# Attention and a mixture of experts on one core: loads, key product and weight splits of the beginning in another order

## What is computed

```
x = x + tanh(g_xattn) * xattn(layernorm(x), context, mask)
x = x + tanh(g_ffn)   * moe(layernorm(x))

xattn: q = hs @ Wq.T + bq; k = ctx @ Wk.T + bk; v = ctx @ Wv.T + bv    (16 heads of 32)
       p = softmax(clip(where(mask, q.k / sqrt(32), -1e4), -50, 50))
       delta = clip(residual_scale, 0, 0.3) * ((p @ v) @ Wo.T + bo)
       layernorm(delta) * gamma + beta
moe:   8 experts, top 2 of softmax(x @ gate.T), renormalised;
       hidden = silu(gate part) * up part (1024), y = hidden @ down.T, sum of weight * y
```

## Time and profile before

| | |
|---|---|
| runs (us) | 964.10, 967.33, 969.12; median 967.33 |
| profiled execution | 964.62 us, span 962.9 us |
| mean granted clock of PE | 0.973 |
| busy, share of the span | PE 94%, DVE 45%, ACT 40%, POOL 27% |
| chain that ended last | PE 76%, issue 6%, POOL 6%, DVE 5%, ACT 3%, DMA 2% |
| moved by DMA | 93.93 MB, mean 98 GB/s |

### The profile page before, as it was taken

How to read it: one execution, slowest core, us unless ns; L and a number is a source line. 1 busy time by engine, 2 the same in 40 slices (tenths; PEclk the granted TensorE clock), 3 DMA queues, 4 the chain that set the end, 5 groups by cost and what they waited for, 6 DMA issues and landing times.

```text
span 962.9 us, 14512 instructions
## 1 busy us (share of the span) xinstructions
PE 903.6 (94%) x4267; PEld 723.8 (75%) x4268; DVE 434.9 (45%) x793; ACT 381.9 (40%) x733; POOL 262.7 (27%) x326
## 2 busy tenths in 40 slices
PE   4977999988789999999999999999999999999994
PEld 3755777766668888888888888888888888888883
DVE  5657868577692122532532534512532163226211
ACT  3565666642522222532532534422532262235221
POOL 6143737363231211211211221311221221112111
PEclk9999999997779999999999999999999999999997
DMA  7210131214744121461361463521361154121121
GB/s 312 88 45 0 60 116 57 74 61 159 265 169 138 33 33 22 121 206 22 117 210 22 118 209 109 207 33 22 110 217 22 33 185 131 30 36 22 27 38 22
DMA packets 27907, 93.93 MB, mean 98 GB/s; under 512 B 5425, under 2 KB 5425, under 8 KB 21105
## 3 DMA queue, kind: packets, MB, share of 16 engines
q1 hardware_dynamic: 18528, 72.03, 20.1%
q0 software_dynamic: 8640, 20.62, 11.7%
q10 hardware_dynamic: 720, 1.07, 0.3%
HBM read 75.03 MB, written 18.68 MB: 97 GB/s over the span
## 4 chain that ended last, share of the span: by engine, by line
PE 76%; issue 6%; POOL 6%; DVE 5%; ACT 3%; DMA 2%; DVEq 0%; SPq 0%; POOLq 0%; ACTq 0%
PE bank L254 69%; PE bank L1442 3%; POOL ex_lo L775 2%; PE bank L1428 2%; DMA xs<-in_x 2%; POOL o_lo L755 1%; POOL xr L759 1%; PE bank L1278 1%; DVE xr L419 1%; ACT hs L929 1%; DVE st_a L359 1%; DVE o_lo L559 0%; PE bank L1272 0%; POOL rs L763 0%; DVE tok_tile L642 0%
## 5 line engine op out<-in xcount | busy, mean ns | idle before, releaser
L254 PE MATMUL bank<-g_hi,gt_hi 128*128 128x512 f32 x592 | 237.5, 401 | 0.9 <-DVE gt_lo L668 0.9
L254 PE MATMUL bank<-g_lo,gt_hi 128*128 128x512 f32 x592 | 234.1, 395 | 0.0
L254 PE MATMUL bank<-g_hi,gt_lo 128*128 128x512 f32 x592 | 234.1, 395 | 0.0
L698 DVE TENSOR_TENSOR hid<-silu,bank 128x256 f32<-128x256 f32 x148 | 61.3, 419 | 307.4 <-ACT silu L1155 307.4
L1155 ACT ACTIVATE silu<-bank 128x256 f32<-128x256 f32 x148 | 56.5, 381 | 253.8 <-PE bank L254 253.8
L887 POOL COPY g_idx<-slot_idx 128x1 int32 x37 | 6.9, 185 | 470.1 <-ACT w_nxt L1169 470.1
L254 PEld LDWEIGHTS bank<-g_hi,gt_lo 128*128 128x128 f32 x592 | 111.3, 188 | 26.9
L254 PEld LDWEIGHTS bank<-g_hi,gt_hi 128*128 128x128 f32 x592 | 111.3, 188 | 26.3 <-issue 1.1
L254 PEld LDWEIGHTS bank<-g_lo,gt_hi 128*128 128x128 f32 x592 | 111.4, 188 | 25.0
L254 PE MATMUL bank<-dn_hi,hd_hi 128*128 128x512 f32 x296 | 126.8, 428 | 0.0
L254 PE MATMUL bank<-dn_hi,hd_lo 128*128 128x512 f32 x296 | 116.9, 395 | 0.0
(11 more groups left out here) (227 smaller groups left out, 1277.9 us busy)
## 6 DMA issues: line engine op xcount, KB each, us to landing
raw<-in_w_exp SPq DMA_DIRECT2D x48, 1024.0 KB, 5.3
raw<-in_w_attn SPq DMA_DIRECT2D x4, 1024.0 KB, 13.1
xs<-in_x SPq DMA_DIRECT2D x4, 1024.0 KB, 6.4
xr<-in_x SPq DMA_DIRECT2D x4, 1024.0 KB, 5.9
out_rows<-xr SPq DMA_DIRECT2D x16, 256.0 KB, 2.2
h_rows<-dh SPq DMA_DIRECT2D x16, 256.0 KB, 2.1
rows<-in_b_rows ACTq DMA_DIRECT2D x1, 1024.0 KB, 11.9
c_raw<-in_ctx_t SPq DMA_DIRECT2D x1, 640.0 KB, 3.9
```

The source lines that it names most:

```text
L254: mm = eng.matmul(psum, a(k), b(k), start=(first and k == 0 and j == 0), stop=(last and k == n - 1 and j == 2))
L698: dve.tensor_tensor(hid[:, p, :], silu[:, p, :], bank[p][:, 256:512], ALU.mult).then_inc(hid_done, 1)
```

## The change

- SP loads the key weights as four chunks of 128 x 512 with a semaphore each. The order is then value weights, xs, query weights, `rows`, output weights. `rows` was on ACT's queue, with the constants; it has its own semaphore now, and the wait for the constants counts four loads.
- ACT and DVE split the key weights chunk by chunk, and PE multiplies chunk by chunk, with four accumulations open at once in banks 0, 1, 6 and 7 (quarters m of the output). The key bias becomes four instructions of 256 columns, and the x transposes into banks 0 and 1 wait for the first two of them.
- PE starts with 36 transposes of the identity into bank 3, as soon as the identity is written; the wait for the rest of POOL's set-up moves behind the key product.
- The x transposes of batch 0 stand behind the third and the fourth value group (before: the first and the second).
- ACT splits the query weights ahead of normalise_x(0) (before: between the halves of x_high), DVE ahead of the value biases (before: after two x_low).
- The products of `rows` with the gates stand behind the first two clips, `bo_two` behind the last q_low of batch 0, and PE waits for it only after batch 0.
- In batch 0 ACT's o_copy(0) and o_copy(1) stand one exponential earlier; the split of the output weights stands behind k_high(1) on ACT, and ahead of v_low(1) and the last two q_low on DVE.

The value weights, the tiles and their sizes, the expert loop and all that is computed stay.

```diff
@@ sync @@
-            for w in range(2):
-                sp.dma_start(raw[:, w, :], w_attn[w]).then_inc(wload[w], 16)
+            for k in range(KC):
+                sp.dma_start(raw[:, 0, k * H:(k + 1) * H], w_attn[0][:, k * H:(k + 1) * H]).then_inc(
+                    wk_load[k - 1] if k else wload[0], 16)
+            sp.dma_start(raw[:, 1, :], w_attn[1]).then_inc(wload[1], 16)
             sp.dma_start(xs[:, :, :], x_b[0]).then_inc(xload, 16)
-            for w in range(2, 4):
-                sp.dma_start(raw[:, w, :], w_attn[w]).then_inc(wload[w], 16)
+            sp.dma_start(raw[:, 2, :], w_attn[2]).then_inc(wload[2], 16)
+            sp.dma_start(rows[:, :, :], b_rows.partition_broadcast(P)).then_inc(row_load, 16)
+            sp.dma_start(raw[:, 3, :], w_attn[3]).then_inc(wload[3], 16)
@@ vector, batch @@
+                if not back:
+                    split_weight(3)
+                if front:
                     v_low(b + 1)
                     q_low(b + 1, 2)
                     q_low(b + 1, 3)
-                if not back:
-                    split_weight(3)
@@ vector, beginning @@
-            split_weight(0)
+            for k in range(KC):
+                dve.wait_ge(wk_h, k + 1)
+                dve.tensor_tensor(wk_lo[:, k, :], raw[:, 0, k * H:(k + 1) * H], f32(wk_hi[:, k, :]),
+                                  ALU.subtract).then_inc(wk_l, 1)
             split_weight(1)
             ln_statistics(0)
...
+            dve.wait_ge(kv_mm, 1)
+            for m in range(KC):
+                kb = dve.tensor_scalar(k_all[:, m, :], k_bank[m][:, 0:NB * T], bcol[:, 1, m:m + 1], None, ALU.add)
+                if m % 2 == 1:
+                    kb.then_inc(kv_sb, 1)
+            split_weight(2)
...
+            dve.wait_ge(row_load, 16)
+            v_bias(0, (NB, 0))
+            x_low(0, 0)
+            x_low(0, 1)
+            v_bias(1, (1,))
@@ scalar, batch @@
                 exps(2)
-                exps(3)
                 if not back:
                     o_copy(0)
+                exps(3)
                 exps(4)
+                if not back:
+                    o_copy(1)
                 exps(5)
-                o_copy(1)
+                if back:
+                    o_copy(1)
...
                     k_high(b + 1)
+                if not back:
+                    split_weight(3)
@@ scalar, beginning @@
-            split_weight(0)
+            for k in range(KC):
+                act.wait_ge(wk_load[k - 1] if k else wload[0], 16)
+                act.activation(wk_hi[:, k, :], raw[:, 0, k * H:(k + 1) * H], ACT.Copy).then_inc(wk_h, 1)
             split_weight(1)
-            act.wait_ge(cload, 80)
+            split_weight(2)
+            act.wait_ge(cload, 64)
             act.activation(tg[:, 0:2], gsc[:, 0:2], ACT.Tanh).then_inc(gates_ready, 1)
             normalise_x(0)
-            x_high(0, range(0, 2))
-            split_weight(2)
-            x_high(0, range(2, KC))
+            x_high(0)
@@ tensor @@
-            pe.wait_ge(setup, 22)
+            pe.wait_ge(setup, 2)
...
+            stay_busy(36, bank[3])
             pe.wait_ge(c_l, 1)
-            pe.wait_ge(w_lo_done, 1)
-            for m in range(KC):
-                mm = product3(pe, bank[6 + m // 2][:, (m % 2) * NB * T:(m % 2 + 1) * NB * T],
...
+            for k in range(KC):
+                pe.wait_ge(wk_l, k + 1)
+                for m in range(KC):
+                    mm = product3(pe, k_bank[m][:, 0:NB * T], lambda _: wk_hi[:, k, m * P:(m + 1) * P],
...
-                if i < 2:
-                    x_transposes(0, range(2 * i, 2 * i + 2))
-            pe.wait_ge(w_lo_done, 3)
+                if i >= 2:
+                    if i == 2:
+                        pe.wait_ge(kv_sb, 1)
+                    x_transposes(0, range(2 * i - 4, 2 * i - 2))
+            pe.wait_ge(w_lo_done, 2)
...
-            pe.wait_ge(bo_done, 3)
             first_part(0)
             batch(0, False, True)
+            pe.wait_ge(bo_done, 3)
```

More of the change, by code:

```diff
@@ L213, in flamingo_gated_block @@
         gates_ready, w_hi_done, w_lo_done = sem("gates_ready"), sem("attn_w_hi"), sem("attn_w_lo")
-        dset = sem("vector_setup")
+        dset, row_load = sem("vector_setup"), sem("bias_rows_loaded")
+        wk_load = [sem(f"key_weight_chunk{k}_loaded") for k in range(1, KC)]
+        wk_h, wk_l = sem("key_weight_hi"), sem("key_weight_lo")
         ln_bias, ln_stats, ln_mean, ln_var, ln_rstd, hs_done = (sem(n) for n in
@@ L256, in product3 @@
             return mm
+        k_bank = (bank[0], bank[1], bank[6], bank[7])
         weight_halves = ((wk_hi[:, :, :], wk_lo[:, :, :]), (wv_hi[:, :, :], wv_lo[:, :, :]),
@@ L347, in split_weight @@
                 hi, lo = (a.rearrange("p k n -> p (k n)") for a in weight_halves[w])
-                dve.wait_ge(w_hi_done, w + 1)
+                dve.wait_ge(w_hi_done, w)
                 if w == 3:
@@ L494, in batch, with v_bias @@
                     q_low(b + 1, 3)
-                if not back:
-                    split_weight(3)
-            split_weight(0)
+            for k in range(KC):
+                dve.wait_ge(wk_h, k + 1)
+                dve.tensor_tensor(wk_lo[:, k, :], raw[:, 0, k * H:(k + 1) * H], f32(wk_hi[:, k, :]),
+                                  ALU.subtract).then_inc(wk_l, 1)
             split_weight(1)
             ln_statistics(0)
-            dve.wait_ge(cload, 80)
+            dve.wait_ge(cload, 64)
             dve.tensor_scalar(tg[:, 2:3], gsc[:, 2:3], 0.0, 0.3, ALU.max, ALU.min).then_inc(dset, 1)
             dve.tensor_scalar(lim[:, :], mask_sb[:, :], 0.5, 2.0 * CLIP, ALU.is_gt, ALU.mult).then_inc(dset, 1)
-            dve.wait_ge(dset, 2)
+            dve.wait_ge(kv_mm, 1)
[4 more added lines that the diff above has]
+            split_weight(2)
+            def v_bias(i, places):
+                dve.wait_ge(kv_mm, i + 2)
+                for place in places:
+                    dve.tensor_tensor(v_all[:, place, :], bank[2 + (place - 1) % NB][:, :], rows[:, 0, :],
+                                      ALU.add).then_inc(kv_sb, 1)
+            dve.wait_ge(row_load, 16)
[3 more added lines that the diff above has]
+            v_bias(1, (1,))
+            x_low(0, 2)
+            x_low(0, 3)
+            v_bias(2, (2,))
+            k_low(0)
+            v_low(0)
+            v_bias(3, (3,))
+            q_low(0, 0)
+            dve.wait_ge(dset, 2)
+            dve.tensor_scalar(lim[:, :], lim[:, :], -CLIP, None, ALU.add).then_inc(dset, 1)
+            dve.wait_ge(dset, 3)
+            q_low(0, 1)
+            clip(0, 0, True)
+            clip(0, 1, True)
             dve.wait_ge(gates_ready, 1)
-            dve.tensor_scalar(lim[:, :], lim[:, :], -CLIP, None, ALU.add).then_inc(dset, 1)
             dve.tensor_scalar(rows[:, 1, :], rows[:, 1, :], tg[:, 2:3], None, ALU.mult).then_inc(dset, 1)
             dve.tensor_scalar(rows[:, 2:4, :], rows[:, 2:4, :], tg[:, 0:1], None, ALU.mult).then_inc(dset, 1)
+            q_low(0, 2)
+            q_low(0, 3)
             dve.wait_ge(dset, 5)
@@ L1358, in batch @@
                     router(b - 1, 3)
+            stay_busy(36, bank[3])
             pe.wait_ge(c_l, 1)
-            pe.wait_ge(w_lo_done, 1)
-            for m in range(KC):
-                mm = product3(pe, bank[6 + m // 2][:, (m % 2) * NB * T:(m % 2 + 1) * NB * T],
[L1365 to L1368, removed]
+            for k in range(KC):
+                pe.wait_ge(wk_l, k + 1)
+                for m in range(KC):
+                    mm = product3(pe, k_bank[m][:, 0:NB * T], lambda _: wk_hi[:, k, m * P:(m + 1) * P],
+                                  lambda _: wk_lo[:, k, m * P:(m + 1) * P], lambda _: c_hi[:, k, 0:NB * T],
+                                  lambda _: c_lo[:, k, 0:NB * T], n=1, first=(k == 0), last=(k == KC - 1))
+            mm.then_inc(kv_mm, 1)
+            pe.wait_ge(setup, 22)
+            pe.wait_ge(w_lo_done, 1)
             for i, n in enumerate(V_ORDER):
```

4 lines of the change are left out of this document (removed).

## The result

The changed kernel takes a median of **959.91 us** (956.43 to 963.53 in 17 runs), the kernel before 964.10 (960.61 to 970.23 in 17 runs) on the same chips. The ratio on record is 0.9945 with a 95% interval of 0.9927 to 0.9962: 5.3 us faster, 3.7 to 7.0; the two medians are 4.2 apart. The measured 959.91 lies inside the range, 2.9 above the predicted 957. But 957 was built on a median of 967.33 from three runs; against 964.10 my sum of 10.0 would have said 954.1, and about half of that gain came. So the sum is what has to be explained. The profiled execution has a span of 958.2 against 962.9.

The account below looks back on a forecast made before the run. TensorE works nearly throughout the expert loop, so only the work before it, where TensorE has holes, can move earlier. 7.2 - 1.8 + 4.6 = 10.0 us gained, from a median of 967.33 to 957; range 951 to 963.

Parts of the forecast that it names:

- I take neither gain nor loss: Loads at the beginning: three more DMA issues ahead of the value weights are hidden by over 1 MB still being moved.
- rival 2: Beginning: xs lands no earlier, hs ends at 25.7 as now, 2.1 us less gained, 959; chance 0.12.
- a sign of being wrong: Beginning: xs, forecast to land near 15.0, landing past 15.5 would show the prediction wrong.
- The clock of the value product: Beginning: value product starts at 15.5, matmuls 0.23 us each; first query product at 30.2 against 37.37, 7.2 us gained.
- The transposes: Start of PE: 36 identity transposes from about 1.7 to 7.0–8.9 us raise the clock; key matmuls then 0.12 apart.
- bo_two: Batch 0, ahead of the clips of scores 2 and 3: clips and all behind follow later, 1.8 us lost, bounds 0 and 2.5.
- the bank is not what is late next: Batch 0: o_copy ahead of exps(3) and exps(5) frees the bank sooner, but ex_lo of score 2 is late next.
- The fourth rival: Batch 0: added wait lengthens PE's holes, its clock falls for the whole batch, 14.6 us more, 972; chance 0.02.
- Output weights: End of batch 0: moving their split brings pv of score 2 of batch 1 4.6 us earlier, bounds 2.0 and 5.0.
- rival 3: End of batch 0: output weights' split only moves the wait; 1.5 of 4.6 us remains, 960; chance 0.13.
- the 1.3 of GpSimd's wait for ex_hi: Output weights' term: GpSimd's 1.31 us wait for ex_hi after o_lo vanishes once PE's hole is gone.
- The 3.3: Output weights' term: PE's 4.02 us hole at the end of batch 0 closes by 2.8 to 3.8, say 3.3 us.

Follow-up runs that it names:

- one load: Changed kernel with the key weights in one load again, splits and product still by chunk; 959.53 us, ratio 0.9933.
- bo_two late: Changed kernel with the three bo_two instructions behind the clips of scores 6 and 7 of batch 0; 959.22 us, ratio 0.9951.
- 20 more: Changed kernel with 20 more identity transposes between key and value product; 961.55 us, ratio 0.9958.
- the constants late: Changed kernel with the four small constant loads moved from ScalarE's queue to SP behind x, chunks kept; 959.72 us, ratio 0.9946.

## Why the prediction was right, and where its sum was not

The direction was right, and the measured time lies in the range. That 957 is only 2.9 off is luck: the base, 967.33, was 3.2 above the median of the kernel before, and this hid more than half of what the sum had too much. The sum was 10.0; of it 3.9 stand at ex_lo in the trace, 5.3 in the ratio and 4.2 in the medians. (The range's own terms, 955 and 961 with 2.5 to either side, give 952.5 to 963.5, not 951 to 963.)

- **The loads.** The step that failed is "I take neither gain nor loss" for the chunks, with its reason that "the over 1 MB that is then still being moved hides them". 57 GB/s between 5 and 7 us show that there was no such cover. The value weights came 2.0 later (one load: 0.0), v0 at 17.59 instead of 15.5. xs landed 11.9 us behind its issue at 3.77, at 15.7: 1.9 sooner than before, so rival 2 falls, but past the 15.5 that I had named as a sign of being wrong. It did not matter, since the statistics stand behind wv_lo on VectorE (17.36, against 15.5 forecast).
- **The clock of the value product.** I watched the clock of the key product and let the value product run at 0.23 throughout. With PE idle for 2.25 us ahead of it, it ran 1.6 longer in this trace. With the 2.1 of the loads this makes 3.7: q0 at 33.85 instead of 30.2. Where the clock stayed up, the interval v0 to q0 was 14.5 to 14.6; I had worked out 14.7.
- **The transposes.** Right as forecast, 5.76 us from 1.61 and 0.12 behind them. But the term carried no microsecond that shows: what it speeds up waits for the value weights. And the row it was read from says less than I took from it: the 0.61 from 252 to 256 us is the mean over the 22 transposes themselves, not of a stretch ahead of them (0.50 from 254 to 255, 0.96 from 255 to 256), and other matmuls stand ahead. The run without transposes shows the effect; the row only allowed it.
- **bo_two.** 1.8 forecast, 1.69 in the trace. Up to batch 1's transposes 2.7 are lost, though: bo_two's 1.6, 0.6 for PE's clock, and 0.6 that remain with bo_two late. That rest is most likely o_copy ahead of exps(3), which I had put at nothing ("the bank is not what is late next"): it makes GpSimd's second ex_lo late. The fourth rival's mechanism is real, in half the traces and at 0.6 instead of 14.6 us.
- **Output weights.** 4.6 forecast, 3.1 to 3.25 in four traces, so rival 3, with 1.5, falls too. Of the two terms, the 1.3 of GpSimd's wait for ex_hi came in full: ex_lo now follows o_lo without a wait. The 3.3 was mis-sized: counted from q1, the spreads behind the hole start 17.29 us later instead of 19.13, 1.8 sooner. What failed is the length of v_low, forecast at 2.28 or half of it: it took 3.31, while GpSimd's two ex_lo beside it took 3.96 instead of 2.60. The hole fell to 0.61, but the one of 1.34 behind vbd_lo stands ahead of it.
- **The rest of the way.** Between ex_lo and the expert loop the lead grew from 3.9 to 4.9 us. The medians of the others do not follow ex_lo in order: the kernel without transposes is 2.1 ahead of that with 20 more in the median, and 1.4 behind it at ex_lo; the profiled span with the constants late was 952.6, its median 959.72. One trace is one execution, and runs of one kernel spread by 7 us; the last batch is where the traces differ most: from the update to the first product of the routing stage they take 57.0 to 63.4 us, with a granted clock between 0.76 and 0.86, and the expert loop behind takes 684.6 to 685.0 in all of them. How often each kernel takes the one or the other no run here counts, so a lead of 1 to 2 us in a trace is not to be read as time.

## What to carry to other kernels

Before a load is cut into chunks, look at what else is in flight on the other queues: here the chunks delayed the load behind them by about as much as the earlier start was worth. A clock that is raised early is worth something only if the engine has no hole before the work that decides; fill to the start of that work and not past it, or bring its data forward. Walk the lead of a new kernel through fixed points of the program (v0, q0, q1, ex_lo) before adding up terms: here a lead of 3.5 us at q0 was 0.8 at q1.

## What the runs showed of the hardware

- Four loads of 128 x 512 on one queue beside four small loads on another: 57 GB/s in the changed kernel between 5 and 7 us, 365 with one load instead, 255 with the small ones moved.
- 36 transposes of the identity, with no other matmul, bring TensorE to its higher level: key matmuls 0.12 apart behind them, 0.21 without.
- Holes of TensorE of 1.78 and 1.94 us left its clock up, holes of 1.99, 2.25 and 2.60 brought it down (granted 0.50 from 11.2 to 14.4 us behind the last), 1.0 to 1.7 us after work had begun again. The length of the hole alone does not tell: holes of 1.17 and 0.97 close together in batch 0 brought it down in four traces and left it up in four, and a hole of 2.3 ahead of batch 1's transposes left it up in four.
- One VectorE instruction of 128 x 512 takes 0.75 us, and 1.73, 2.97 or 4.23 where it has to let one, two or three instructions of GpSimd (1.3 each) go first.
